# Routing weight rows by wide products, and FFN block 5's down side stacked in its idle rows

## The chip, the cores and the metric

The kernel runs on one core of a Trainium2 chip. The metric is the device time of one execution in microseconds. Engines: TensorE (PE), VectorE (DVE), ScalarE (ACT), GpSimd (POOL) and SyncE (SP, which only issues the loads and stores).

## What is computed

The reference is a four-stage transformer step on x of 1024 x 256 in fp32; every stage adds its output to x:

```python
x = x + attention(layernorm(x))
x = x + ffn(layernorm(x))
x = x + mixer(layernorm(x))      # state-space mixer
x = x + ffn(layernorm(x))        # the same weights as the first
```

The FFN is a mixture of 8 LoRA experts over one dense FFN with 704 hidden units. Each token picks the two experts with the highest router logits; the softmax that weighs them runs over all tokens of a choice (axis 1), so it needs a maximum and a sum over all 1024 tokens:

```python
topw, sel = top_k(x @ gate_w.T, 2)
topw = softmax(topw, axis=1)                     # over the tokens
for e in range(8):
    c = sum(where(sel == e, topw, 0.0))
    h_e = silu(base_up + lo_up[e]) * (base_gate + lo_gate[e])
    ch = c * h_e
    mixed_h += ch
    lora_down += 2 * (ch @ down_A[e].T @ down_B[e].T)
out = mixed_h @ w_down.T + lora_down
```

## The kernel before

All four stages are written out instruction by instruction for each engine, with semaphores between them; there is no planner. Engines run their own queues in the order in which the code issues to them. The FFN is built twice by `ffn(tag, first, before)`, for stage 2 and stage 4; only the first time are its weights split.

**Precision.** An fp32 product is made of three fp32r products: each operand is split into a high part (rounded to fp32r) and a low part (the remainder), and `three()` (L170 issues all its products) adds high x high, high x low and low x high. ACT writes high parts, DVE low ones.

**Tiling.** The 704 hidden units are cut into HB = 6 blocks of 128, the tokens into two halves of 512. A step i = 0..11 is one block in one half, i = HB * half + block. Block 5 has only 64 real units. Its up and gate results share one PSUM bank (`to_bank`): rows 0 to 63 up, rows 64 to 127 gate, so its base stage has 6 products in place of 12. ACT moves silu to rows 64 to 127, and the down weights of block 5 lie in rows 64 to 127 with zeros in rows 0 to 63. It is called packed.

**A step on PE.** `base_x(i)`: 12 products of 512 columns (up and gate, two halves of the model dimension, three terms). `base_lora(i)`: 6 products that add the first choice's LoRA; `second(i)`: 6 that add the difference between the second and the first choice's LoRA on top, once the first choice has been read. `down(i)`: for each of the two slots (choices) 3 products of 512 columns with down_A, and for each of 4 token tiles 3 products of 256 columns with w_down. Loop over i: base_x(i), base_lora(i), second(i-1), down(i-2). In step 8 lora_down(0) stands between second and down, and down(6) waits for the residual add of half 0.

**A step on ACT and DVE.** For each slot s: silu on ACT (L1140), `gated` on DVE (L1243, t = gate * silu, reads PSUM), `slot` (L1299, ch = t * weights wb), ACT's high part of ch (L1158), DVE's low part (L1310); then mix = ch of slot 0 + ch of slot 1 (L1306), its high part (L1169) and low part (L1318). base_x(i) waits for gated(i-2, 1). DVE also makes, in between, the masked LoRA inputs `masked` (L1255, 8 for each half, those of half 1 in steps 5 and 6), in the first FFN the low parts of the weights (`split`, L878), and in steps 8 to 12 work for the next stage (statistics and normalisation of half 0, low parts of the mixer's weights).

**Routing weights.** The chain is `top` on DVE, a transpose, a maximum, two small products on PE, exp on ACT, a sum on PE (L1037), reciprocal and product on DVE (L1283): WT, 128 x 16, one column for each slot and token tile. `weigh(h)` (L1018) spreads it over the partitions: one fp32 product of 128 columns for each slot and tile, with a column of WT as the stationary operand, broadcast to 128 columns, and the identity as the moving one; 8 a call, each two records in the trace. ACT copies the two banks to wb (`weights_out`, L1149). weigh(0) follows second(0), weigh(1) follows base_x(2).

**GpSimd** has in the FFN only the reciprocal square roots of the layer norms (L224).

Of the kernel before, what the change touches and what calls it, by code (L numbers as in the profile page):

```python
# [20 lines left out]
F32 = mybir.dt.float32  # L21
# [63 lines left out]
PR_END = PR_CS + 26  # L85
# [17 lines left out]
def build(nc, ins, out, phases=4):  # L103
    ctx = ExitStack()
    with ctx:
# [166 lines left out]
        def attention():  # L272
# [511 lines left out]
            def banks_free(e):  # L784
# [15 lines left out]
        s_fwh, s_fwl = sem("ffn_w_hi"), sem("ffn_w_lo")  # L800
# [6 lines left out]
        F_EVENTS = dict(lg=2, lgt=2, lgr=2, lgc=2, m8=NT, ix=NT, ixf=2, hot=4, top_dve=6, top_pe=3, ex=SLOTS,  # L807
                        wb=4, wbc=4, u=4, uhi=4, ulo=4, mk=4, mk0=2, mk1=2, mk2=2, um=16,
                        da=4, dd0=4, dd=4, dh=4, dl=4, y=4, add=4)
        F_EVENTS |= {n: 2 * HB for n in "a b d sil0 sil1 t0 t1 ch0 ch1 mix mxh mxl".split()} | dict(chh=4 * HB, chl=4 * HB)  # L810
        FS = {n: sem(f"ffn_{n}") for n in F_EVENTS}
        TOP_DVE = {n: i + 1 for i, n in enumerate(("mt", "gm", "dg", "nmc", "rs", "wt"))}
        TOP_PE = {n: i + 1 for i, n in enumerate(("mtT", "nm", "sum"))}

        def ffn(tag, first, before):
# [16 lines left out]
            d_hl = at(f"{tag}_d_hl", [P, 2, HALF], F32R, U_CH + 18432)  # L832
            lg = small[:, 0:64]
# [5 lines left out]
            WT = sm[:, 32:48].rearrange("p (k t) -> p k t", k=2)  # L839
# [116 lines left out]
            MASK_STEP = HB - 2  # L956

# [16 lines left out]
            def to_bank(i, which):  # L974
                return bank(i % 2 if i % HB == HB - 1 else 2 * which + i % 2)

            def base_x(e, i, parts=(0, 1)):
                h, b = divmod(i, HB)
# [21 lines left out]
            def pe(e):  # L1000
                def second(i):
                    h, b = divmod(i, HB)
                    if b == 0:
# [7 lines left out]
                def weigh(h):  # L1011
                    need(e, "top_dve", TOP_DVE["wt"])
# [25 lines left out]
                base_lora(e, 0)  # L1038
                base_lora(e, 1)
# [3 lines left out]
                def down(i):  # L1043
                    h, b = divmod(i, HB)
# [55 lines left out]
            def act(e):  # L1100
# [26 lines left out]
                split(3)  # L1127
                a_hi(1, (0,))
# [5 lines left out]
                def silu(i, s):  # L1134
# [3 lines left out]
                    packed = i % HB == HB - 1  # L1138
# [1076 lines left out]
```

## Time and profile before

| | us |
|---|---|
| Median of 3 runs (lowest to highest) | 546.32 (546.05 to 546.50) |
| The profiled execution, its own time | 543.31 |
| Its span in the trace | 541.50 |
| PE busy | 517.0 |
| DVE busy | 402.6 |
| ACT busy | 310.8 |
| POOL busy | 127.1 |

The stages by the timeline of PE, from the span's start: attention to about 207 us, the first FFN to 331, the mixer to 420, the second FFN to the end. In a row of a timeline the first number is the start, the second the length; a bracket gives the idle time of that engine before it and what ended it. Neighbouring instructions of a kind are merged (x12 is twelve of them). PE's ends are modelled and overlap what follows, so its pace is read from start to start.

### The profile page before, as it was taken

How to read it: one execution, taken by the hardware profiler on the slowest of the kernel's cores; microseconds unless marked ns; L12 is line 12 of the kernel's file. 1: busy time of each engine (PE TensorE's matmuls, PEld its weight loads, DVE VectorE, ACT ScalarE, POOL GpSimd, SP SyncE). 2: the span in 40 equal slices, each digit the busy share in tenths (PEclk: the TensorE clock that was granted, in tenths of full speed). 3: DMA queues.
4: the chain of work that ended last, by engine and by line, in shares of the span. 5: the costliest groups of instructions: out<-in, count | busy, mean ns of one | idle time of the engine just before them, and what ended most of it. 6: DMA issues, size and time to landing. Idle time of an engine off the chain costs nothing. (4 is left out here: it accounts for less than half of the span.)

```text
span 541.5 us, 9132 instructions
## 1 busy us (share of the span) xinstructions
PE 517.0 (95%) x3035; PEld 436.8 (81%) x3037; DVE 402.6 (74%) x899; ACT 310.8 (57%) x768; POOL 127.1 (23%) x272
## 2 busy tenths in 40 slices
PE   5999999999999989999999999999898999999996
PEld 4778899998998977788887888757777778888885
DVE  5625565566566898799987899966886877898767
ACT  3656878588687643573443455889662254443342
POOL 2232424244243310000000004569533100000000
PEclk9999999999999999999999999999999999999999
DMA  7320100000002204000040000000000000000101
GB/s 273 116 79 1 40 2 2 2 0 2 2 2 70 83 1 142 1 1 1 0 137 0 2 1 0 2 0 2 0 1 2 0 1 1 1 1 0 40 1 39
DMA packets 5790, 14.25 MB, mean 26 GB/s; under 512 B 624, under 2 KB 2928, under 8 KB 5744
## 3 DMA queue, kind: packets, MB, share of 16 engines
q1 hardware_dynamic: 5744, 13.66, 7.3%
q8 instruction: 25, 0.41, 0.3%
q14 instruction: 21, 0.17, 0.1%
HBM read 12.61 MB, written 1.05 MB: 25 GB/s over the span
## 5 line engine op out<-in xcount | busy, mean ns | idle before, releaser
L170 PE MATMUL psum<-xT_hl,ffn_w_hl 128*128 128x512 f32 x312 | 77.7, 395 | 0.6 <-DVE f_t L1243 0.4
L170 PE MATMUL psum<-f_um,ffn_w_hl 128*128 128x512 f32 x288 | 72.2, 398 | 1.3 <-DVE f_t L1243 1.3
L170 PEld LDWEIGHTS psum<-xT_hl,ffn_w_hl 128*128 128x128 f32 x312 | 56.2, 188 | 12.2 <-issue 0.9
L170 PEld LDWEIGHTS psum<-f_um,ffn_w_hl 128*128 128x128 f32 x288 | 53.3, 188 | 14.2 <-DVE f_um L1255 2.1
L1140 ACT ACTIVATE f_sil<-psum 128x512 f32<-128x512 f32 (+1 forms) x48 | 28.6, 596 | 60.3 <-PE psum L170 60.0
L170 PE MATMUL psum<-wo_hl,oT_hl 128*128 128x256 f32 x384 | 50.8, 281 | 4.2 <-DVE oT_hl L705 2.6
L699 DVE TENSOR_TENSOR pT_hl<-psum,pT_hl 126x360 fp32r<-126x360 f32 (+1 forms) x44 | 23.6, 537 | 41.4 <-ACT pT_hl L606 41.4
L170 PEld LDWEIGHTS psum<-wo_hl,oT_hl 128*128 128x128 f32 x384 | 47.9, 188 | 7.1 <-DVE oT_hl L705 5.1
L170 PE MATMUL psum<-xT_hl,wq_hl 128*128 128x512 f32 x192 | 52.1, 407 | 0.6 <-ACT qT L572 0.6
L1243 DVE TENSOR_TENSOR f_t<-psum,f_sil 128x512 f32<-128x512 f32 (+1 forms) x48 | 33.2, 691 | 26.2 <-ACT f_sil L1140 25.4
L572 ACT ACTIVATE qT<-psum 128x512 f32<-128x512 f32 x32 | 35.0, 1094 | 29.0 <-PE psum L170 29.0
L1158 ACT ACTIVATE f_ch_hl<-f_ch 128x512 fp32r<-128x512 f32 x48 | 30.2, 630 | 37.0 <-DVE f_ch L1299 36.9
L581 ACT ACTIVATE probs<-probs,small 120x66 f32<-120x66 f32 x120 | 40.7, 349 | 4.2 <-DVE small L682 3.4
L170 PEld LDWEIGHTS psum<-xT_hl,wq_hl 128*128 128x128 f32 x192 | 33.9, 189 | 7.7 <-issue 1.7
L170 PEld LDWEIGHTS psum<-ffn_w_hl,f_mix_hl 128*128 128x128 f32 x288 | 36.8, 188 | 3.3 <-DVE x_resid L1342 1.2
L170 PE MATMUL psum<-f_ch_hl,ffn_w_hl 128*128 128x512 f32 x144 | 37.9, 397 | 0.6 <-DVE f_ch_hl L1310 0.6
L170 PE MATMUL psum<-ffn_w_hl,f_mix_hl 128*128 128x256 f32 x288 | 37.7, 280 | 0.5 <-DVE x_resid L1342 0.5
L755 POOL TENSOR_TENSOR probs_wide<-probs,small 120x186 f32<-120x186 f32 x40 | 20.0, 499 | 65.8 <-DVE small L662 65.5
L224 POOL TENSOR_TENSOR ln_rstd<-ln_var_eps,minus_half 128x4 f32<-128x4 f32 x8 | 8.1, 1012 | 113.9 <-DVE ln_var_eps L217 113.9
L1299 DVE TENSOR_TENSOR f_ch<-f_t,f_wb 128x512 f32<-128x512 f32 x48 | 33.2, 691 | 1.4
L170 PEld LDWEIGHTS psum<-f_ch_hl,ffn_w_hl 128*128 128x128 f32 x144 | 26.6, 188 | 7.0 <-DVE f_ch_hl L1310 1.0
L1310 DVE TENSOR_TENSOR f_ch_hl<-f_ch,f_ch_hl 128x512 fp32r<-128x512 f32 x48 | 31.1, 686 | 0.0
(242 smaller groups left out, 1121.4 us busy)
## 6 DMA issues: line engine op xcount, KB each, us to landing
w_raw<-in_wq SPq DMA_DIRECT2D x4, 512.0 KB, 3.3
w_raw<-in_wo SPq DMA_DIRECT2D x4, 512.0 KB, 3.3
ffn_w_raw<-in_ffn SPq DMA_DIRECT2D x3, 576.0 KB, 5.6
ffn_w_raw_far<-in_ffn SPq DMA_DIRECT2D x3, 576.0 KB, 5.2
ssd_w_raw<-in_ssd SPq DMA_DIRECT2D x3, 512.0 KB, 5.7
x_resid<-in_x SPq DMA_DIRECT2D x2, 512.0 KB, 4.4
out_x<-x_resid SPq DMA_DIRECT2D x4, 256.0 KB, 2.2
w_raw<-in_wk SPq DMA_DIRECT2D x1, 512.0 KB, 6.3
```

What stands on the lines that cost most here:

```text
L170: i = e.matmul(dst, lhs(a), rhs(b), start=start and n == 0, stop=stop and n == len(TERMS) - 1, **kw)
L224: e.tensor_tensor(rstd[:, seg], veps[:, seg], minus_half[:, seg], ALU.pow).then_inc(LN["rstd"], 1)
L572: e.activation(qT[:, HALF * half:HALF * half + HALF, h], bank(7 if n == Q_PAIR else 6), ACT.Copy, scale=float(HD) ** -0.5).then_inc(s_qt, 1)
L581: m = e.activation(p[:, n, :], p[:, n, :], ACT.Exp, bias=NEGM[0:rows, u % 4, n:n + 1], accum_out=DEN[0:rows, u % 4, n:n + 1])
L699: e.tensor_tensor(pT_hl[0:nk, u % 2, LO, 0:n], bank(2 + u % 2)[0:nk, 0:n], f32(pT_hl[0:nk, u % 2, HI, 0:n]), ALU.subtract).then_inc(s_plo, 1)
L755: e.tensor_tensor(wide, p[:, :, SINK:KBLK], spread(r, KB_WIN), ALU.mult)
L1140: e.activation(sil[at_rows, s, :], bank(i % 2)[rows, :], ACT.Silu).then_inc(FS[f"sil{s}"], 1)
L1158: e.activation(ch_hl[:, i % 2, s, HI, :], ch[:, i % 2, s, :], ACT.Copy).then_inc(FS["chh"], 1)
L1243: e.tensor_tensor(tt[rows, s, :], to_bank(i, 1)[rows, :], sil[rows, s, :], ALU.mult).then_inc(FS[f"t{s}"], 1)
L1299: e.tensor_tensor(ch[:, i % 2, s, :], tt[:, s, :], wb[:, s, half(h)], ALU.mult).then_inc(FS[f"ch{s}"], 1)
L1310: e.tensor_tensor(ch_hl[:, i % 2, s, LO, :], ch[:, i % 2, s, :], f32(ch_hl[:, i % 2, s, HI, :]), ALU.subtract).then_inc(FS["chl"], 1)
```

## The change

**Weight rows.** DVE writes the weights repeated over 128 columns (w_rep); PE transposes them in one transpose, between base_lora(0) and base_lora(1); ACT copies the result (wr) and DVE subtracts it in the rows where the low part belongs (so wr holds high parts in some rows and low parts in others, by a column of parameters). For each half the rows are then spread into wr_rhs, four 128x128 products with a column of parameters, on ACT for half 0 and on POOL for half 1. slot_rows are two constant 128x128 tiles, made by ACT. weigh(h) becomes one product of 512 columns for each slot.

**Order of DVE around it.** masked(0, 4, 5), then the subtract, gated(0, 0), and only then masked(0, 6, 7); second(0) waits for the former before its first three products and for the latter before its other three.

**Block 5's down side.** Its down weights stand in both halves of the rows. Rows 0 to 63 of the high part are overwritten, once, with the low parts (ACT, at step 4 of the first FFN). POOL zeroes rows 0 to 63 of t before the step, and copies ch and mix from rows 64 to 127 into rows 0 to 63 of the low tiles. So two products in place of three give all three terms: the down products of block 5 are 2 x 2 and 4 x 2 in place of 2 x 3 and 4 x 3.

**Order of blocks.** In half 1: 0, 1, 2, 5, 3, 4; packed steps are 5 and 9 in place of 5 and 11.

**Waits.** base_x(i) waits, before its up products, only for silu(i-2, 1), unless step i-2 is packed, and for gated(i-2, 1) before its gate products. DVE's slot(i) waits in packed steps for the zeroing, and slot and mixed two steps later for POOL's copies; down in packed steps waits for them too. In the mixer two semaphores are merged into others, with the same waits.

The core of the diff:

```diff
+            ORDER = list(range(HB)) + [0, 1, 2, HB - 1] + list(range(3, HB - 1))
+            PACKED = [i for i in range(N) if ORDER[i] == HB - 1]
 def to_bank(i, which):
-    return bank(i % 2 if i % HB == HB - 1 else 2 * which + i % 2)
+    return bank(i % 2 if i in PACKED else 2 * which + i % 2)
 def base_x(e, i, parts=(0, 1)):
-                if i >= 2:
-                    need(e, "t1", i - 1)
                 for which in parts[:1] if b == HB - 1 else parts:
+                    if i >= 2:
+                        need(e, "t1" if which or i - 2 in PACKED else "sil1", i - 1)
 def second(i):
-                    if b == 0:
-                        need(e, "um", 8 * h + 8)
+                    if i % HB == 0:
+                        need(e, "um", 8 * h + 6)
                     need(e, "t0", i + 1)
                     for which in range(2):
+                        if i % HB == 0 and which:
+                            need(e, "um", 8 * h + 8)
 def weigh(h):
-                        for i in range(HT):
-                            t = HT * h + i
-                            m = e.matmul(bank(wb_bank(h, s))[:, i * P:(i + 1) * P],
-                                         WT[:, s, t:t + 1].broadcast_to([P, P]), ident, start=True, stop=True)
-                        m.then_inc(FS["wb"], 1)
+                        e.matmul(bank(wb_bank(h, s)), slot_rows[:, s, :], wr_rhs[:, h].rearrange("p t n -> p (t n)"),
+                                 start=True, stop=True).then_inc(FS["wb"], 1)
 # PE, start of the FFN
                 base_lora(e, 0)
+                need(e, "top_dve", TOP_DVE["wt"])
+                e.transpose(bank(7)[:, 2 * P:3 * P], w_rep, ident).then_inc(FS["top_pe"], 1)
                 base_lora(e, 1)
 def down(i):
+                        if i in PACKED:
+                            if s == 0:
+                                e.wait_ge(s_fwx, 1)
+                            need(e, "cx", 2 * h + s + 1)
+                            for w in (HI, LO):
+                                m = e.matmul(bank(6 + s), blk(HI, b, FB_DA, ER), ch_hl[:, i % 2, s, w, :],
+                                             start=False, stop=closes and w == LO)
...
+                        if i in PACKED:
+                            for w in (HI, LO):
+                                m = e.matmul(bank(4 + t // 2)[:, (t % 2) * D:(t % 2 + 1) * D],
+                                             mix_hl[:, i % 2, w, t * P:(t + 1) * P], blk(HI, b, FB_DN, D),
+                                             start=False, stop=False, skip_group_check=True)
+                            continue
 # ACT, start of the FFN
                 a_hi(1, (1,))
+                need(e, "top_pe", TOP_PE["wT"])
+                e.activation(wr, bank(7)[:, 2 * P:3 * P], ACT.Copy).then_inc(FS["wrh"], 1)
                 silu(0, 0)
+                need(e, "top_dve", TOP_DVE["wlo"])
+                for t in range(HT):
+                    m = e.activation(wr_rhs[:, 0, t, :], f32(wr), ACT.Copy, scale=par[:, WR_HALF + t:WR_HALF + t + 1])
+                m.then_inc(FS["wr0"], 1)
 # DVE, start of the FFN
-                masked(0, 4, 5, 6, 7)
+                masked(0, 4, 5)
+                need(e, "wrh", 1)
+                e.scalar_tensor_tensor(out=wr, in0=f32(wr), scalar=par[:, CS_LO:CS_LO + 1], in1=bank(7)[:, 2 * P:3 * P],
+                                       op0=ALU.mult, op1=ALU.add).then_inc(FS["top_dve"], 1)
                 gated(0, 0)
+                masked(0, 6, 7)
 def pool(e):
                 ln["rstd"](e, 1)
+                need(e, "top_dve", TOP_DVE["wlo"])
+                for t in range(HT):
+                    m = e.tensor_scalar(wr_rhs[:, 1, t, :], f32(wr), par[:, WR_HALF + HT + t:WR_HALF + HT + t + 1], None,
+                                        ALU.mult)
+                m.then_inc(FS["wr1"], 1)
+
+                def zeros(h, s):
+                    need(e, f"ch{s}", PACKED[h])
+                    e.memset(tt[0:REST, s, :], 0.0).then_inc(FS["z"], 1)
+
+                def stacked_rows(h):
+                    i = PACKED[h]
+                    need(e, "z", 2 * h + 2)
+                    need(e, "d", i - 1)
+                    for s in range(SLOTS):
+                        need(e, f"ch{s}", i + 1)
+                        e.tensor_copy(ch_hl[0:REST, i % 2, s, LO, :], ch[REST:P, i % 2, s, :]).then_inc(FS["cx"], 1)
+                        need(e, "cx", 2 * h + s + 1)
+                    need(e, "mix", i + 1)
+                    e.tensor_copy(mix_hl[0:REST, i % 2, LO, :], mix[REST:P, i % 2, :]).then_inc(FS["mx"], 1)
+                    need(e, "mx", h + 1)
+
+                zeros(0, 0)
+                zeros(0, 1)
+                stacked_rows(0)
+                zeros(1, 0)
                 early(phase, "rstd0", e)
+                zeros(1, 1)
+                stacked_rows(1)
```

## Rows read from the trace of the kernel before

**Rows 1.** Page: busy us, share of span, instructions of each engine

```profile
PE 517.0 (95%) x3035; PEld 436.8 (81%) x3037; DVE 402.6 (74%) x899; ACT 310.8 (57%) x768; POOL 127.1 (23%) x272
```

**Rows 2.** Windows, first FFN: length, busy PE, PEld, DVE, ACT, POOL; clock

```profile
236.00:330.00 94.00, 93.09 (x489) 78.15 (x488) 83.23 (x148) 43.06 (x76) 1.01 (x1) 1.00 0.06 20
```

**Rows 3.** Timeline of PE, an ordinary block: start us, length us

```profile
240.29 2.93 PE L170 MATMUL psum<-xT_hl,ffn_w_hl 128*128 128x512 f32 x12
243.06 2.96 PE L170 MATMUL psum<-f_um,ffn_w_hl 128*128 128x512 f32 x12
245.86 1.56 PE L170 MATMUL psum<-f_ch_hl,ffn_w_hl 128*128 128x512 f32 x6
247.26 1.56 PE L170 MATMUL psum<-ffn_w_hl,f_mix_hl 128*128 128x256 f32 x12
248.66 2.89 PE L170 MATMUL psum<-xT_hl,ffn_w_hl 128*128 128x512 f32 x12
```

**Rows 4.** Timeline of PE, second FFN: weigh(0) and what comes after it

```profile
441.01 1.95 PE L1018 MATMUL psum<-const_f,softmax_small 128*128 128x128 f32 x16
442.71 3.01 PE L170 MATMUL psum<-xT_hl,ffn_w_hl 128*128 128x512 f32 x12
```

**Rows 5.** Groups by line, transposes: busy us, mean ns, idle before

```profile
L238 PE MATMUL psum<-const_f,xn 128*128 128x128 f32 x24 | 3.7, 287 | 0.1
```

**Rows 6.** Page, costliest groups: DVE's low parts of ch

```profile
L1310 DVE TENSOR_TENSOR f_ch_hl<-f_ch,f_ch_hl 128x512 fp32r<-128x512 f32 x48 | 31.1, 686 | 0.0
```

**Rows 7.** Timeline, second FFN's start: gated(0,0) on DVE, second(0) on PE

```profile
438.71 0.69 DVE L1243 TENSOR_TENSOR f_t<-psum,f_sil 128x512 f32<-128x512 f32 x1
439.54 1.63 PE L170 MATMUL psum<-f_um,ffn_w_hl 128*128 128x512 f32 x6 [0.66 <-DVE f_t L1243]
```

**Rows 8.** Timelines of DVE and PE, first FFN

```profile
229.19 0.69 DVE L1243 TENSOR_TENSOR f_t<-psum,f_sil 128x512 f32<-128x512 f32 x1 [1.19 <-ACT f_sil L1140]
...
236.04 0.69 DVE L1318 TENSOR_TENSOR f_mix_hl<-f_mix,f_mix_hl 128x512 fp32r<-128x512 f32 x1 [0.31 <-ACT f_mix_hl L1169]
...
253.62 0.69 DVE L1243 TENSOR_TENSOR f_t<-psum,f_sil 128x512 f32<-128x512 f32 x1 [0.45 <-ACT f_sil L1140]
...
271.77 0.69 DVE L1243 TENSOR_TENSOR f_t<-psum,f_sil 64x512 f32<-64x512 f32 x1
...
272.91 2.89 PE L170 MATMUL psum<-xT_hl,ffn_w_hl 128*128 128x512 f32 x12
...
277.87 0.69 DVE L1243 TENSOR_TENSOR f_t<-psum,f_sil 128x512 f32<-128x512 f32 x1 [2.08 <-ACT f_sil L1140]
...
290.31 1.68 PE L170 MATMUL psum<-ffn_w_hl,f_mix_hl 128*128 128x256 f32 x12 [0.48 <-DVE x_resid L1342]
...
300.75 3.00 PE L170 MATMUL psum<-xT_hl,ffn_w_hl 128*128 128x512 f32 x12 [0.43 <-DVE f_t L1243]
```

**Rows 9.** Timelines of DVE and PE, second FFN

```profile
457.94 0.69 DVE L1243 TENSOR_TENSOR f_t<-psum,f_sil 128x512 f32<-128x512 f32 x1 [2.18 <-ACT f_sil L1140]
...
484.42 0.70 DVE L1243 TENSOR_TENSOR f_t<-psum,f_sil 64x512 f32<-64x512 f32 x1
...
485.56 2.89 PE L170 MATMUL psum<-xT_hl,ffn_w_hl 128*128 128x512 f32 x12
...
533.00 0.96 PE L170 MATMUL psum<-f_ch_hl,ffn_w_hl 128*128 128x512 f32 x3 [0.59 <-DVE f_ch_hl L1310]
```

**Rows 10.** Groups by line and shape on POOL, the mixer

```profile
L2010 POOL TENSOR_SCALAR mask_f32r<-const_f 128x512 fp32r<-128x512 f32 x1 | 0.6, 617 | 0.1
...
L1971 POOL TENSOR_SCALAR xs_D<-xs,params 128x512 f32<-128x512 f32 x6 | 9.9, 1642 | 0.0
...
L2022 POOL TENSOR_SCALAR cumsum_sel<-cumsum_hl,params 128x128 fp32r<-128x128 f32 x8 | 3.6, 447 | 0.0
```

**Rows 11.** Timeline, mixer: a GpSimd product and DVE's g_lo

```profile
378.32 1.05 POOL L2046 TENSOR_TENSOR x_dt_decay<-x_dt,decay 128x512 f32<-128x512 f32 x1
378.61 1.30 DVE L1908 TENSOR_TENSOR g_lo<-gated,g_hi 128x512 fp32r<-128x512 f32 x1 [0.87 <-ACT g_hi L1838]
```

More of the change, by code:

```diff
@@ L832, in ffn @@
             d_hl = at(f"{tag}_d_hl", [P, 2, HALF], F32R, U_CH + 18432)
+            wr = at(f"{tag}_weight_rows", [P, P], F32R, A_W + 16384)[:, :]
+            w_rep = at(f"{tag}_weights_repeated", [P, P], F32, A_W + 16896)[:, :]
+            slot_rows = at(f"{tag}_slot_rows", [P, SLOTS, P], F32R, A_W + 17408)
+            wr_rhs = at(f"{tag}_weight_rows_rhs", [P, 2, HT, P], F32R, A_W + 20480)
             lg = small[:, 0:64]
@@ L1047, in down @@
                         need(e, "ulo", 4)
-                    if h == 1 and b == 0:
+                    if h == 1 and opens:
                         need(e, "dd0", 2)
@@ L1127, in act @@
                 split(3)
+                for n in range(SLOTS):
+                    e.activation(slot_rows[:, n, :], ones, ACT.Copy, scale=par[:, WR_SLOT + n:WR_SLOT + n + 1])
                 a_hi(1, (0,))
@@ L1198, in act @@
                         split(6, 7)
+                    if i == MASK_STEP and first:
+                        e.wait_ge(s_fwl, HB + 1)
+                        stacked = slice(F_BLK + (HB - 1) * FB + FB_DN, F_BLK + HB * FB)
+                        e.activation(w_hl[0:REST, HI, stacked], f32(w_hl[0:REST, LO, stacked]),
+                                     ACT.Copy).then_inc(s_fwx, 1)
                     if i == N - 5:
@@ L1240, in gated @@
                         need(e, f"ch{s}", i)
-                    packed = i % HB == HB - 1
+                    packed = i in PACKED
                     rows = slice(REST, P) if packed else slice(0, P)
@@ L1309, in lo_slot @@
                     need(e, "chh", 2 * i + s + 1)
-                    e.tensor_tensor(ch_hl[:, i % 2, s, LO, :], ch[:, i % 2, s, :], f32(ch_hl[:, i % 2, s, HI, :]),
-                                    ALU.subtract).then_inc(FS["chl"], 1)
+                    rows = slice(REST, P) if i in PACKED else slice(0, P)
+                    e.tensor_tensor(ch_hl[rows, i % 2, s, LO, :], ch[rows, i % 2, s, :],
+                                    f32(ch_hl[rows, i % 2, s, HI, :]), ALU.subtract).then_inc(FS["chl"], 1)
                 def lo_parts(i):
@@ L1317, in lo_parts @@
                     need(e, "mxh", i + 1)
-                    e.tensor_tensor(mix_hl[:, i % 2, LO, :], mix[:, i % 2, :], f32(mix_hl[:, i % 2, HI, :]),
-                                    ALU.subtract).then_inc(FS["mxl"], 1)
+                    rows = slice(REST, P) if i in PACKED else slice(0, P)
+                    e.tensor_tensor(mix_hl[rows, i % 2, LO, :], mix[rows, i % 2, :],
+                                    f32(mix_hl[rows, i % 2, HI, :]), ALU.subtract).then_inc(FS["mxl"], 1)
                 def lora_mask(h):
@@ L2177, in pack @@
                     blocks(padh(eb(a["ffn_up_B"]), 1), P), blocks(behind(eb(a["ffn_gate_B"]), 1), P),
[L2178 to L2179 removed]
+                    kmaj(twice(a["ffn_w_down"])).transpose(1, 0, 2),
+                    kmaj(twice(er(a["ffn_down_A"]))).transpose(1, 0, 2))
     ffn = [kmaj(er(a["ffn_up_A"])), kmaj(er(a["ffn_gate_A"]))] + [w for b in per_block for w in b] + [eb(a["ffn_down_B"])]
```

94 lines of the change are left out of this document (58 added, 36 removed).

## The prediction, made before the changed kernel was run

> **What bounds the kernel now.** I read the page's engine table first: TensorE (PE) is busy 95% of the span, VectorE (DVE) 74% [rows 1]. A share says nothing of single stages, so I took the table by windows: from 236 to 330 us, nearly all of the first FFN, PE is busy 93.09 of 94.00 us and DVE 83.23 [rows 2]. PE bounds it, but DVE is close behind. The timeline of PE then shows how work is paced. One ordinary block is 12 base products, 12 LoRA products, 6 down-A products and 12 down products, back to back with no idle note: 2.77, 2.80, 1.40 and 1.40 us from start to start [rows 3]. So a product with 512 columns costs 0.233 us and one with 256 columns 0.117. The clock is 1.00 in the window [rows 2], the 2.4 GHz level, and the change makes no pause in PE long enough that I expect that to differ.
>
> **What leaves PE.** (a) Weight rows: weigh() is 8 fp32 products of 128 columns, 16 in the records, and takes 442.71 - 441.01 = 1.70 us [rows 4]; there are four such calls, two in each FFN. After, each is two 512-column products: 2 x 0.233 = 0.47. Saved 4 x 1.23 = 4.9 us. (b) New are two transposes of 128x128; 24 such take 3.7 us [rows 5], so 0.15 each, 0.3 together. (c) Block 5's down side: per half two products of 512 columns and four of 256 fall away, 0.47 + 0.47 = 0.93; four halves make 3.7 us. (d) Order 0,1,2,5,3,4 in half 1: block 5's short base stage (6 products, 1.4 us less) comes two iterations earlier; the sum is unchanged. PE would save 4.9 - 0.3 + 3.7 = 8.3 us. My forecast is far less, because much of this lands where DVE or a chain through it sets the time.
>
> **FFN start.** The transpose goes in after base_lora(0); behind it on ACT come the copy into wr, silu(0,0) and four copies that make wr_rhs for half 0; on DVE the subtract for the low rows (an op of DVE with two SBUF inputs and 512 columns occupies 31.1/48 = 0.65 us [rows 6], so 128 columns at most that) waits for that copy. Queued behind the subtract is gated(0,0), which PE's second(0) waits for. Today gated(0,0) starts at 438.71 right behind four masked products and second(0) at 439.54 after 0.66 idle [rows 7]. Tomorrow only two masked products precede it (1.3 less), the subtract and the ACT detour are added (up to 1.3 more): I leave it at its time, with bounds -1.3 and +0.7. The other two masked products come behind it: ready at 438.71 + 0.69 + 1.3 = 440.7, whereas PE has done three of six products at 439.54 + 0.70 = 440.24. PE waits 0.4, so second(0) and gated(0,1), which follows it through ACT's silu, come 0.4 later. base_x(2) came 1.70 after second(0), with weigh(0) between; now it waits, in its first half, for silu(0,1) alone, some 0.8 after second(0) (0.65 as for such an op, and the hand-over), so it starts 0.9 - 0.4 = 0.5 earlier. Two constant copies on ACT (slot_rows), the one copy that stacks block 5's low weights and the four for half 0's rows find room: ACT is busy 43.06 of 94.00 us [rows 2]; without that room they cost up to 0.65 each. The parameter load grows by ten columns, at a point where nothing waits for it; no load is added.
>
> **First FFN.** DVE runs without idle from gated(0,1) at 229.19 to gated(4,0), but for 0.31 at 236.04 (waiting for ACT) and 0.45 at 253.62 (waiting for silu) [rows 8]. PE's 2 x 1.23 arrive early at a DVE that can't start earlier: DVE is 0.4 late, wins 0.31 (weights_out(1) leaves ACT earlier) and 0.45, net 0.35, and then runs full until gated(5,1) at 271.77, for which base_x(7) waits; that today starts 0.45 after it ends (272.91 - 272.46) [rows 8]. So at base_x(7) PE gains 0.8, not 2.4. Here silu's earlier release doesn't help, because block 5 holds both its results in one bank. Next, down(5) is 0.93 shorter, but the down stage of iteration 8 already waits 0.48 for the residual add of DVE (290.31) [rows 8]; it will wait 1.4. Still 0.8. The 0.43 stall before base_x(10) (gated(8,1), 300.75) goes, as the first half needs only silu: 1.2. The early base stage lends 1.4 and takes it back at base_x(11). down(9)'s 0.93 does count, for DVE started that stretch 1.4 earlier: 2.2 us at the end of this FFN. It is then carried through the mixer unchanged: only semaphore names differ there.
>
> **Second FFN.** No weight splits here, so DVE idles 2.18 before gated(3,0) [rows 9]. PE keeps 1.23 (weigh(1)) + 0.5 (base_x(2)) = 1.75. base_x(7) starts at 485.56, 0.44 after gated(5,1) ends (485.12) [rows 9], and both shift alike. down(5)'s 0.93 goes into the wait for add(0), as in the first. down(9)'s goes too: the tail is a DVE chain from gated(11,0) on, and PE already waits 0.59 for its last ch_hl at 533.00 [rows 9]. So 1.75. Together 3.95 us if GpSimd's new work is free.
>
> **What GpSimd's work costs.** Each packed half adds two memsets (64x512) and three copies (64x512, crossing partitions); each FFN start adds four products of 128x128. No row has a copy across partitions. The nearest one-input op with 512 columns took 0.617 us, the same with a scalar per partition 1.64 [rows 10]; I take 0.62 and keep 1.64 as the bound (below, 0.3: half of it, as half the partitions). A 128x128 product takes 0.447 [rows 10]. Waits of DVE for them (ch(7), mixed(7), ch(11)) and of PE's down(5), down(9) come an iteration later and are covered by over 2 us, but engines also collide: DVE's g_lo, two SBUF inputs, started at 378.61 while GpSimd's product from 378.32 to 379.37 ran, and took 1.30 against 0.69 for such an op; it ended 0.54 after GpSimd did [rows 6, 11]. So DVE stands still until GpSimd has finished. The Trainium skill ("SBUF — State Buffer", Who interferes with whom) has it as an exclusive lock: a DVE op with two SBUF inputs and a GpSimd op that reads SBUF block each other fully, whichever started second; that row agrees. The new memsets only write and by the same section don't collide; no row here shows it.
>
> Nearly all DVE ops around the new copies have two SBUF inputs. Where DVE is a full chain, a block costs the whole op: in each FFN start two masked products may be held by 0.45 each; in the first FFN the first copy of half 0 (0.62) is in the chain, and of half 1 two copies (1.24), of which 0.6 is covered (DVE's lead of 1.4 less down(9)'s 0.93, and some hand-over); those after step 5 meet the 2.08 before 277.87 [rows 8]; in the second FFN the first copy meets 0.44 of slack (0.18), and the others meet idle time. Fully blocked: 0.9 + 0.9 + 0.62 + 0.64 + 0.18 = 3.2. Never blocked: 0. No row says who wins when DVE has the next op waiting, so I take one hit of two: 0.45 + 0.45 + 0.3 + 0.1 + 0 = 1.3. Forecast: 3.95 - 1.3 = 2.65 us. The profiled run took 543.31 (span 541.5), 3.0 below the median of 546.32; subtracted from the median this gives 543.7.
>
> **Rivals.**
> *PE keeps its saving* (0.12): the DVE waits dissolve because ops shift by fractions. For it: PE is 99% busy in [rows 2]. Against: DVE's chain in [rows 8] is unbroken. 5 to 8.3 us: 538.0 to 541.3, middle 539.7.
> *Every copy blocks* (0.14): 3.95 - 3.2 = 0.75, 545.6. The rule of the page above, a lock for the whole op, would give this if GpSimd always comes in between two DVE ops.
> *The copy across partitions is dear* (0.07), slower: with c per copy and full blocking, 3.95 - 1.8 leaves 2.15; the chain copies cost 3c - 0.6 in the first FFN and c - 0.44 in the second, so the gain is 3.2 - 4c. It turns at c = 0.8, and at 1.64 [rows 10] is -3.4: 549.7.
> *It doesn't do what it says* (0.05): second(0) waits for masked products and ACT for as long as weigh saves: 546.3.
> The forecast has 0.62.
>
> **Numbers.** Measurement can tell about 0.2%, 1.1 us. Faster: 0.62 + 0.12 + 0.03 of the full-block case (parts of it under 545.2) = 0.77; same: 0.11 + 0.05 = 0.16; slower 0.07. The range runs from 541.0 (forecast without any collision, 542.4, and a little of the first rival) to 546.3 (takes in full blocking and the last rival).
>
> **What would show it.** L1018's 64 records gone, four pairs of 512-column products at about 0.47 a call; 3.7 us less of down products. PE's idle grows at second(0) (0.4 for f_um), base_x(7) and the adds (about 1.4), and at 533 (1.5); DVE's ch, mixed and lo ops, always 0.69 today, show some of 1.0 to 1.3 beside GpSimd's copies. If PE has no such new idle, the DVE part of my reading is wrong; if copies last over 1 us, their price is.

## The result, and the profile of the changed kernel

Six runs of each kernel: before 545.10 us (median; three of the six are those that the forecast started from), after 539.02 us, ratio 0.9897 (95%: 0.9874 to 0.9921). The forecast was 543.7, range 541.0 to 546.3. The direction was right; the gain was larger than forecast, and the time lies below the range. Runs of either kernel come at two levels, 1.4 to 2.5 us apart (the last section shows where part of that arises), and those three runs all lay on the upper one; so I compare traces first. The profiled run took 538.82 us against 543.31 with full clock in both, and the spans differ by 541.5 - 537.0 = 4.5 us. Forecast: 2.65.

The page's engine line and two groups of after, to hold against [rows 1] and [rows 6]; the third is the new zeroing on POOL:

```profile
PE 510.3 (95%) x2957; PEld 427.7 (80%) x2959; DVE 407.6 (76%) x901; ACT 313.3 (58%) x783; POOL 149.5 (28%) x300
...
L1367 DVE TENSOR_TENSOR f_ch_hl<-f_ch,f_ch_hl 128x512 fp32r<-128x512 f32 (+1 forms) x48 | 35.6, 779 | 0.1
...
L1463 POOL MEMSET f_t<- 64x512 f32 x8 | 4.2, 520 | 101.6 <-DVE f_ch L1353 101.6
```

PE is busy for 6.7 us less, DVE for 5.0 more. 4.5 of that is one group: the low parts of ch, 31.1 us in [rows 6], now 35.6, though not one was added and some cover half the partitions. That is the collision with GpSimd, sized below.

The timeline of PE at the first FFN's start (start us, length us, engine, line, operation, count, and in brackets the idle time before it and what ended it):

```profile
226.58 0.94 PE L172 MATMUL psum<-f_um,ffn_w_hl 128*128 128x512 f32 x3 [0.27 <-DVE f_t L1284]
227.78 0.96 PE L172 MATMUL psum<-f_um,ffn_w_hl 128*128 128x512 f32 x3 [0.27 <-DVE f_um L1296]
228.58 0.61 PE L1028 MATMUL psum<-f_weight_rows_rhs,f_slot_rows 128*128 128x512 f32 x2
229.52 3.01 PE L172 MATMUL psum<-xT_hl,ffn_w_hl 128*128 128x512 f32 x12 [0.33 <-ACT f_sil L1170]
232.37 0.62 PE L1028 MATMUL psum<-f_weight_rows_rhs,f_slot_rows 128*128 128x512 f32 x2
232.83 1.56 PE L172 MATMUL psum<-f_um,ffn_w_hl 128*128 128x512 f32 x6
```

Weigh costs 232.83 - 232.37 = 0.46 us (forecast 0.47; 1.70 in [rows 4]). second(0) waits once for gated(0,0) and once for the masked inputs, and base_x(2), which is now held by silu alone, waits 0.33. Around block 5 and the two steps that follow it:

```profile
271.72 3.00 PE L172 MATMUL psum<-xT_hl,ffn_w_hl 128*128 128x512 f32 x12 [0.53 <-DVE f_t L1284]
274.56 2.96 PE L172 MATMUL psum<-f_um,ffn_w_hl 128*128 128x512 f32 x12
277.36 1.10 PE L1069 MATMUL psum<-f_ch_hl,ffn_w_hl 128*128 128x512 f32 x4
278.30 1.09 PE L1084 MATMUL psum<-ffn_w_hl,f_mix_hl 128*128 128x256 f32 x8
279.23 2.89 PE L172 MATMUL psum<-xT_hl,ffn_w_hl 128*128 128x512 f32 x12
...
285.71 1.65 PE L172 MATMUL psum<-ffn_w_hl,f_d_hl 128*128 128x256 f32 x12 [0.79 <-DVE f_d_hl L1393]
...
289.23 1.67 PE L172 MATMUL psum<-ffn_w_hl,f_mix_hl 128*128 128x256 f32 x12 [0.47 <-DVE x_resid L1400]
```

down(5) takes 279.23 - 277.36 = 1.87 instead of 2.80, as forecast. Its 0.93 turns into idle time at once: 0.79 + 0.47 = 1.26 before the two products that wait for DVE in step 8, where [rows 8] has 0.48 (I forecast 1.4).

DVE and POOL in the same stretch:

```profile
264.35 1.70 DVE L1367 TENSOR_TENSOR f_ch_hl<-f_ch,f_ch_hl 128x512 fp32r<-128x512 f32 x2
...
270.88 0.69 DVE L1284 TENSOR_TENSOR f_t<-psum,f_sil 64x512 f32<-64x512 f32 x1
271.61 0.69 DVE L1353 TENSOR_TENSOR f_ch<-f_t,f_wb 128x512 f32<-128x512 f32 x1
272.39 0.69 DVE L1362 TENSOR_TENSOR f_mix<-f_ch 128x512 f32<-128x512 f32 x1
273.11 2.01 DVE L1367 TENSOR_TENSOR f_ch_hl<-f_ch,f_ch_hl 64x512 fp32r<-64x512 f32 x2
```

```profile
225.70 4.26 POOL L1457 TENSOR_SCALAR f_weight_rows_rhs<-f_weight_rows,params 128x128 fp32r<-128x128 f32 x4 [15.47 <-DVE f_weight_rows L1332]
...
264.29 0.61 POOL L1471 CAST f_ch_hl<-f_ch 64x512 fp32r<-64x512 f32 x1
272.43 1.12 POOL L1471 CAST f_ch_hl<-f_ch 64x512 fp32r<-64x512 f32 x1 [7.53 <-DVE f_ch L1353]
273.62 0.96 POOL L1474 CAST f_mix_hl<-f_mix 64x512 fp32r<-64x512 f32 x1
```

For the whole study I cut the span into three stages by PE's timeline: the first FFN from its first base product to the first z product of the mixer, the mixer to the first LoRA product of the second FFN, and that to the last group of LoRA down products. Before: 119.72, 109.25, 100.67. After: 117.47, 109.09, 98.68. So the gain is 2.25 + 0.16 + 1.99.

### The profile page after: what moved, and what is told of

It reads as the page before. It is cut to its first block and busy times, and to the rows that moved or that the text cites. A ratio compares the mean times of both kernels' runs of the same rounds, so it can differ in the third digit from the quotient of the medians.

```text
span 537.0 us, 9053 instructions
## 1 busy us (share of the span) xinstructions
PE 510.3 (95%) x2957; PEld 427.7 (80%) x2959; DVE 407.6 (76%) x901; ACT 313.3 (58%) x783; POOL 149.5 (28%) x300
## 3 DMA queue, kind: packets, MB, share of 16 engines
HBM read 12.62 MB, written 1.05 MB: 25 GB/s over the span
## 5 line engine op out<-in xcount | busy, mean ns | idle before, releaser
L1367 DVE TENSOR_TENSOR f_ch_hl<-f_ch,f_ch_hl 128x512 fp32r<-128x512 f32 (+1 forms) x48 | 35.6, 779 | 0.1
L172 PEld LDWEIGHTS psum<-ffn_w_hl,f_mix_hl 128*128 128x128 f32 x240 | 30.7, 188 | 3.6 <-DVE x_resid L1400 1.8
L172 PE MATMUL psum<-f_ch_hl,ffn_w_hl 128*128 128x512 f32 x120 | 31.7, 398 | 1.1 <-DVE f_ch_hl L1367 1.1
L1463 POOL MEMSET f_t<- 64x512 f32 x8 | 4.2, 520 | 101.6 <-DVE f_ch L1353 101.6
L172 PE MATMUL psum<-ffn_w_hl,f_mix_hl 128*128 128x256 f32 x240 | 31.5, 280 | 0.9 <-DVE x_resid L1400 0.9
L172 PE MATMUL psum<-pT_hl,v_hl 126*128 126x360 f32 (+1 forms) x132 | 30.4, 339 | 0.0
```

Of the source, the lines that this page charges most:

```text
L172: i = e.matmul(dst, lhs(a), rhs(b), start=start and n == 0, stop=stop and n == len(TERMS) - 1, **kw)
L1367: e.tensor_tensor(ch_hl[rows, i % 2, s, LO, :], ch[rows, i % 2, s, :], f32(ch_hl[rows, i % 2, s, HI, :]), ALU.subtract).then_inc(FS["chl"], 1)
L1463: e.memset(tt[0:REST, s, :], 0.0).then_inc(FS["z"], 1)
```

## The experiments

Each was timed beside the kernel before. The table has the ratio to it with its interval, and the stages in us from one profile each. A star marks a profile in which the clock was low at the end of the mixer; the FFN stages aren't touched by that and are what I compare.

| run | ratio (95%) | first FFN | mixer | second FFN |
|---|---|---|---|---|
| c_after | 0.9912 (0.9895-0.9930) | 117.49 | 109.20 | 98.71 |
| x_no_pool_reads | 0.9902 (0.9880-0.9924) | 116.61 | 110.62* | 98.33 |
| x_copies_doubled | 0.9958 (0.9944-0.9973) | 118.57 | 110.82* | 99.07 |
| w_weigh_only | 0.9920 (0.9902-0.9938) | 117.48 | 109.33 | 98.75 |
| s_stack_only | 0.9973 (0.9956-0.9990) | 118.66 | 110.71* | 100.52 |
| r_no_early_release | 0.9970 (0.9951-0.9988) | 119.14 | 110.69* | 99.42 |
| e_release_only | 1.0006 (0.9988-1.0023) | 119.04 | 110.88* | 100.68 |
| w_no_release | 0.9961 (0.9941-0.9982) | 119.19 | 110.84* | 99.49 |
| o_natural_order | 1.0000 (0.9979-1.0021) | 119.31 | 110.84* | 100.52 |
| m_masked_first | 0.9932 (0.9908-0.9957) | 117.96 | 109.14 | 99.07 |
| v_act_copies | 0.9898 (0.9881-0.9915) | 116.69 | 109.08 | 98.46 |
| v_defer | 0.9895 (0.9872-0.9917) | 116.12 | 109.15 | 97.68 |
| v_act_defer | 0.9868 (0.9849-0.9888) | 115.27 | 109.17 | 97.44 |
| v_act_defer_mask | 0.9854 (0.9830-0.9877) | 115.06 | 110.61* | 97.54 |

c_after is the changed kernel again: its FFN stages come out within 0.03 us of the first profile's, the only measure here of how far two profiles of one kernel differ.

> The changed kernel itself once more, beside the kernel before on one chip, as the base of the comparisons. The two traces differ by 4.5 us in their spans, the first ratio says 5.6 with an interval from 4.3 to 6.9. If the spans tell the truth, the ratio comes out near 0.9917 (4.5 us less); if there is a gain that the traces don't show, near 0.990.

The ratio, 0.9912, is 4.8 us less than before. That is near the 4.5 of the traces (0.9917); its interval just takes in 0.990 too. The 0.9897 above leans on the three high runs of before.

**GpSimd without reads.** The copies and the four products become memsets of the same size, so POOL still works but reads nothing. Left out by that: block 5's low terms on the down side and half 1's routing weights.

```diff
-e.tensor_copy(ch_hl[0:REST, i % 2, s, LO, :], ch[REST:P, i % 2, s, :])
+e.memset(f32(ch_hl[0:REST, i % 2, s, LO, :]), 0.0)
...
-m = e.tensor_scalar(wr_rhs[:, 1, t, :], f32(wr), par[...], None, ALU.mult)
+m = e.memset(f32(wr_rhs[:, 1, t, :]), 1.0)
```

> GpSimd's three copies of each packed block and its four products of each FFN start are replaced by memsets of the same tiles with the same waits, so it reads nothing there; the low terms of block 5 and half 1's routing weights are left out. By the collisions as the prediction charged them (1.3 us in all, up to 3.2) this is at least 1.3 us faster than the changed kernel. By the trace of the changed kernel, where DVE lost 0.1 at each FFN start and 0.41 + 0.72 at each packed block, most of it ahead of an idle stretch of DVE, it is 0.3 to 0.8 faster.

DVE and POOL of this run, in the stretch shown above:

```profile
265.15 1.29 DVE L1367 TENSOR_TENSOR f_ch_hl<-f_ch,f_ch_hl 128x512 fp32r<-128x512 f32 x2
...
273.51 1.29 DVE L1367 TENSOR_TENSOR f_ch_hl<-f_ch,f_ch_hl 64x512 fp32r<-64x512 f32 x2
```

```profile
272.81 0.52 POOL L1470 MEMSET f_ch_hl<- 64x512 f32 x1 [7.21 <-DVE f_ch L1353]
273.60 0.52 POOL L1473 MEMSET f_mix_hl<- 64x512 f32 x1 [0.27 <-DVE f_mix L1362]
```

The second pair of low parts starts 0.09 before a memset and takes 1.29, where it took 2.01 beside a copy; the first takes 1.29 instead of 1.70. So a write alone doesn't hold DVE, and a copy, which also reads, does: 0.41 + 0.72 for each packed block. Over the four packed blocks that is 4.5 us of DVE's time, all that the group of low parts grew by. Little of it reaches the end: the first FFN gets 117.47 - 116.61 = 0.86 shorter, the second 98.68 - 98.33 = 0.35. The collisions cost 1.2 us, against 1.3 charged, and more than the 0.3 to 0.8 that I expected of this run. And the gain without them is 3.11 + 2.34 = 5.45 (from 119.72 and 100.67), not 3.95. So a term failed in the part that I took for certain.

**Copies twice.** Each copy is issued twice, each with its own count.

```diff
 e.tensor_copy(ch_hl[0:REST, i % 2, s, LO, :], ch[REST:P, i % 2, s, :])
+need(e, "cx", 2 * (2 * h + s) + 1)
+e.tensor_copy(ch_hl[0:REST, i % 2, s, LO, :], ch[REST:P, i % 2, s, :])
```

> Each of GpSimd's copies in a packed block is done twice. If the copies cost the time that the prediction charged for full blocking (0.62 each where DVE is a full chain), this is 1.4 us or more slower than the changed kernel, for four chain copies are added. If DVE loses only parts that idle stretches take up again, 0.2 to 0.8 slower.

1.10 us longer in the first FFN and 0.39 in the second, 1.5 together: what full blocking asks for (1.4 or more), and not the 0.2 to 0.8 of a DVE that makes up for it. PE shows it where base_x(7) waits for gated of block 5, 0.53 in the changed kernel:

```profile
272.38 1.85 PE L172 MATMUL psum<-xT_hl,ffn_w_hl 128*128 128x512 f32 x7 [0.95 <-DVE f_t L1284]
```

The two runs agree: a copy costs time mainly in the first FFN, where DVE is nearly full, some 0.9 to 1.1 for six of them, and 0.4 in the second.

**One part of the change alone.** w_weigh_only keeps the wide weight rows and silu's early release, but block 5 stays last with three-term products, and POOL zeroes and copies nothing. s_stack_only has weigh, WT and the masked order of before; it stacks block 5 and keeps the new block order and the early release.

```diff
# w_weigh_only
-ORDER = list(range(HB)) + [0, 1, 2, HB - 1] + list(range(3, HB - 1))
+ORDER = 2 * list(range(HB))
...
-if i in PACKED:
+if False:
...
# s_stack_only
-e.matmul(bank(wb_bank(h, s)), slot_rows[:, s, :], wr_rhs[:, h]...)
+m = e.matmul(bank(wb_bank(h, s))[:, i * P:(i + 1) * P], WT[:, s, t:t + 1].broadcast_to([P, P]), ident, ...)
...
-masked(0, 4, 5) ... gated(0, 0); masked(0, 6, 7)
+masked(0, 4, 5, 6, 7); gated(0, 0)
```

> Only the wide weight rows, with the order of work around them and the earlier bank release; block 5's down side and the block order are as before. If PE bounds everywhere, 4.6 us less than before (4 x 1.23 less two transposes). By the DVE chain: 0.8 to 1.2 at base_x(7) of the first FFN, 0.4 at base_x(10), 1.8 in the second FFN, so 3.0 to 3.5 us less than before.

> Only block 5's stacked down side, the order 0,1,2,5,3,4 in half 1 and the earlier bank release; the weight rows by narrow products as before. If PE bounds everywhere: 4 x 0.93 = 3.7 us less than before. By the DVE chains: the 0.93 of down(5) goes into the wait for the residual add in both FFNs, that of down(9) counts in the first FFN alone, and the stall at base_x(10) goes (0.4), less what the first copy costs: 0.8 to 1.4 us less than before.

Weigh with the release gives 2.24 + 1.92, nearly all that the whole change gives (2.25 + 1.99) and above the 3.0 to 3.5 expected by the DVE chain. Stacking with the release gives 1.06 + 0.15; the release alone gives 0.68 and -0.01 (e_release_only, below), so stacking and its order have 0.38 + 0.16 of that. On top of weigh, stacking adds 0.01 + 0.07: its own saving (without POOL's reads 117.48 - 116.61 = 0.87 and 98.75 - 98.33 = 0.42) is about what the collisions, 0.86 + 0.35, take back.

**Silu's early release.** The up products of base_x wait for gated again.

```diff
-need(e, "t1" if which or i - 2 in PACKED else "sil1", i - 1)
+need(e, "t1", i - 1)
```

> The changed kernel with base_x waiting for gated(i-2, 1) before its first product, as before. My working gives the earlier release 0.5 us at base_x(2) and 0.4 at base_x(10) of the first FFN, and 0.5 at base_x(2) of the second, of which the first is lost to the DVE chain: 0.8 to 1.0 us slower than the changed kernel. If the release is worth nothing, as the 1.3 us of idle before these products in the trace of before suggests for single waits, under 0.3.

```profile
231.24 2.97 PE L172 MATMUL psum<-xT_hl,ffn_w_hl 128*128 128x512 f32 x12 [1.05 <-DVE f_t L1284]
...
240.83 2.52 PE L172 MATMUL psum<-xT_hl,ffn_w_hl 128*128 128x512 f32 x10 [0.55 <-DVE f_t L1284]
```

base_x(2) waits 1.05 instead of 0.33, base_x(3) 0.55 where it waited for nothing, and base_x(10) has its wait back (0.54; 0.43 in [rows 8]). The stages lose 1.67 + 0.74 = 2.4 us. That is more than I gave it (0.9 at base_x(2), less 0.4, and 0.43 at base_x(10)). Two more runs settled how they combine: the release added to the kernel before, and taken from w_weigh_only.

```diff
# e_release_only, on before
-if i >= 2:
-    need(e, "t1", i - 1)
 for which in parts[:1] if b == HB - 1 else parts:
+    if i >= 2:
+        need(e, "t1" if which or (i - 2) % HB == HB - 1 else "sil1", i - 1)
# w_no_release, on w_weigh_only: the edit of r_no_early_release
```

> The kernel before with the earlier bank release alone. The trace of before has 0.43 of idle ahead of base_x(10) in the first FFN and none of over 0.1 ahead of the other base products. If the release is worth what those idle notes say, 0.4 us in the first FFN and nothing in the second. If it starts PE's products of a whole chain earlier by itself, over 1 us.

> Only the wide weight rows, without the earlier release (block 5 and the order as before). If the two parts are worth what they are worth alone, the FFNs are 0.4 us longer together than with the release (4.2 us less than before), so 3.8 less. If the release is what lets PE use the time that the weight rows save, because base_x(2) and base_x(3) otherwise wait for gated(0, 1) and gated(1, 1), about 2.4 us longer than with it: 1.8 us less than before, which is what the changed kernel without it showed.

By stages: the release alone gives 0.68 and nothing (0.01 longer), wide rows alone 0.53 + 1.18, the two together 2.24 + 1.92. So 1.03 and 0.75 us exist only with both. Weigh stood between second(0) and base_x(2) and covered the wait for gated(0,1); shorter, it lays the wait bare, as w_no_release shows, and only the release then turns the saving into time:

```profile
230.83 2.99 PE L172 MATMUL psum<-xT_hl,ffn_w_hl 128*128 128x512 f32 x12 [1.04 <-DVE f_t L1282]
```

This base_x(2) stands 23.37 us behind the FFN's start, 0.17 later than in the kernel before, in spite of the 1.23 saved; base_x(3) is 0.47 earlier, and 1.88 earlier in the changed kernel.

**Order.** Block 5 stays last in half 1.

```diff
-ORDER = list(range(HB)) + [0, 1, 2, HB - 1] + list(range(3, HB - 1))
+ORDER = 2 * list(range(HB))
# POOL: the zeroing for half 1 moves behind the layer norm's root
+early(phase, "rstd0", e)
 zeros(1, 0)
-early(phase, "rstd0", e)
```

> The changed kernel with block 5 last in half 1 (packed steps 5 and 11). If the order matters: in the tails down(11) then waits for copies behind the last mix, and its shorter products stand in a stretch that DVE bounds, so 0.9 us of the first FFN's gain goes and up to 1 us is added in the second, 0.9 to 2 us slower than the changed kernel. If the order is free, within 0.3.

The tail of this run, and below it that of after:

```profile
534.37 0.73 PE L1069 MATMUL psum<-f_ch_hl,ffn_w_hl 128*128 128x512 f32 x2 [1.65 <-DVE f_ch_hl L1367]
535.39 1.21 PE L1084 MATMUL psum<-ffn_w_hl,f_mix_hl 128*128 128x256 f32 x8 [0.29 <-DVE f_mix_hl L1376]
538.17 1.64 PE L172 MATMUL psum<-ffn_w_hl,f_d_hl 128*128 128x256 f32 x12 [1.57 <-DVE f_d_hl L1393]
```

```profile
528.74 0.96 PE L172 MATMUL psum<-f_ch_hl,ffn_w_hl 128*128 128x512 f32 x3 [0.82 <-DVE f_ch_hl L1367]
...
532.12 1.64 PE L172 MATMUL psum<-ffn_w_hl,f_d_hl 128*128 128x256 f32 x12 [0.99 <-DVE f_d_hl L1393]
```

The stages are 1.84 us longer in each FFN (119.31 - 117.47, 100.52 - 98.68), 3.7 together, where I expected 0.9 to 2. w_weigh_only has block 5 last too, without stacking, and is as short as the changed kernel; so it is not the short block in the last place that costs, but the stacked one (119.31 - 117.48 and 100.52 - 98.75). DVE's last two low parts of this run show why:

```profile
533.33 0.99 DVE L1367 TENSOR_TENSOR f_ch_hl<-f_ch,f_ch_hl 64x512 fp32r<-64x512 f32 x1
534.24 1.10 DVE L1376 TENSOR_TENSOR f_mix_hl<-f_mix,f_mix_hl 64x512 fp32r<-64x512 f32 x1
```

In the last block everything hangs on DVE's chain. POOL's copies run beside these two (such operations take 0.69 elsewhere), and PE, with 0.93 less to do in the packed down stage, only waits longer. Behind them DVE reaches the last step before the final products here, and in w_weigh_only, at:

```profile
535.37 1.29 DVE L1384 SCALAR_TENSOR_TENSOR f_dd<-psum,f_mT 128x512 f32<-128x512 f32 x2
```

```profile
529.95 1.29 DVE L1376 SCALAR_TENSOR_TENSOR f_dd<-psum,f_mT 128x512 f32<-128x512 f32 x2
```

Counted from the start of this stage (437.65 and 434.00) that is 97.72 against 95.95, 1.77 later and all of the stage's loss. Of it 0.30 + 0.41 are the two rows above, 0.41 the copy before them (the pair of low parts takes 1.70), 0.2 was there at base_x(11), and about 0.35 is an idle stretch ahead of a mix that I haven't taken apart. My sum gave the order down(9)'s 0.93 in the first FFN and some cover for the copies, and nothing in the second; otherwise it "lends 1.4 and takes it back".

**Masked products first.** masked(0, 6, 7) in front of gated(0, 0), as in the kernel before.

```diff
-gated(0, 0)
 masked(0, 6, 7)
+gated(0, 0)
```

> The changed kernel with masked(0, 6, 7) ahead of gated(0, 0) again. Then second(0) starts 1.3 - 0.1 later but runs through: PE's two waits of 0.27 become one. By the chain through silu(0,1) the start of DVE's full stretch moves by the difference, 0.0 to 0.3 us later in each FFN: 0.1 to 0.6 slower. If the order of these is what gave the second FFN its gain, over 1 us slower.

```profile
228.46 1.63 PE L172 MATMUL psum<-f_um,ffn_w_hl 128*128 128x512 f32 x6 [1.25 <-DVE f_t L1284]
```

One wait of 1.25 instead of two of 0.27; the stages lose 0.49 and 0.39, more together than the 0.1 to 0.6 expected. So splitting the waits pays.

**Could it be better?** Three edits follow from the readings: the copies on ACT, behind mix's high part, instead of POOL; down(6) in two stages, its down_A part ahead of lora_down(0) and its w_down part behind base_x(9), so that the wait for the residual add is covered; and the masked inputs of half 1 made behind that step's low parts.

```diff
# v_act_copies, in ACT's step; stacked_rows taken from POOL
+if i in PACKED:
+    for s in range(SLOTS):
+        e.activation(ch_hl[0:REST, i % 2, s, LO, :], ch[REST:P, i % 2, s, :], ACT.Copy)
+    e.activation(mix_hl[0:REST, i % 2, LO, :], mix[REST:P, i % 2, :], ACT.Copy)
# v_defer, in PE's loop
 base_x(e, i)
+if i == HB + 3: down(HB, (1,))
...
 if i == HB + 2:
+    down(HB, (0,))
     lora_down(0)
...
-if i >= 2:
+if i >= 2 and i != HB + 2:
     down(i - 2)
# v_act_defer: both. v_act_defer_mask: both, and in DVE's loop
-if i == MASK_STEP + 2: masked(1, 4, 5, 6, 7)
 ... lo_parts(i - 1)
+if i == MASK_STEP + 2: masked(1, 4, 5, 6, 7)
```

> The changed kernel with the three copies of each packed block on ACT in place of GpSimd; the memsets and the four products of each FFN start stay on GpSimd. With the copies replaced by memsets the first FFN was 0.9 us and the second 0.4 us shorter than in the changed kernel, of which 0.1 each came from the four products. If it is the collision of GpSimd's reads with DVE that costs, this regains 0.8 to 1.1 us. If it is DVE waiting for the copied rows, or if ACT's extra 2 us per packed block come in the way of silu, it regains nothing or loses up to 1 us.

> The changed kernel with PE's order around the residual add changed: down(6)'s first part ahead of lora_down(0), its second part after base_x(9). The trace of the changed kernel has PE idle 0.79 + 0.47 there in the first FFN and about 0.1 + 0.48 in the second. If the add is what holds PE, and the 0.93 saved by down(5) is lost in it, this is 1.2 to 1.8 us faster, as base_x(9) fills the wait. If DVE's chain behind it sets the time anyway, under 0.3.

> Both of these together. If they are separate losses they add up: 2.0 to 2.9 us faster than the changed kernel. If both lie on one DVE chain, only the larger of the two.

> And, beyond both, DVE's masked(1, 4, 5, 6, 7) moved from ahead of gated(6, 0) to behind the low parts of step 5. base_x(7) then no longer waits 0.5 in the first FFN; second(6) needs the masked products about 4 us later. If that chain is what took the early gain of the weight rows (1.9 us at base_x(6), 1.2 at base_x(7)), another 0.2 to 0.6 us. If the products now come too late for second(6), it is slower by up to 1 us.

Against c_after the stages gain 0.80 + 0.25 by the copies on ACT, nearly what taking all reads away gave (0.88 + 0.38); DVE's low parts of ch are back at 31.1 us in all (35.6 in after), so ACT's copies cost DVE nothing. They gain 1.37 + 1.03 by the deferred down and 2.22 + 1.27 by both, more than the 1.8 and 2.9 that I expected at most. PE's timeline of v_act_defer has no idle note where after waited 0.79 and 0.47 (nor the 0.53 before base_x(7)):

```profile
282.73 2.96 PE L172 MATMUL psum<-f_um,ffn_w_hl 128*128 128x512 f32 x12
285.53 1.56 PE L172 MATMUL psum<-f_ch_hl,ffn_w_hl 128*128 128x512 f32 x6
286.93 1.56 PE L172 MATMUL psum<-ffn_w_hl,f_d_hl 128*128 128x256 f32 x12
288.33 1.53 PE L172 MATMUL psum<-xT_hl,ffn_w_hl 128*128 128x512 f32 x6
290.00 1.67 PE L172 MATMUL psum<-ffn_w_hl,f_mix_hl 128*128 128x256 f32 x12
```

The masked order adds 0.21 in the first FFN and costs 0.10 in the second: no difference can be claimed. v_act_defer (0.9868) and v_act_defer_mask (0.9854) have the lowest ratios of the study; v_act_defer's interval lies below c_after's 0.9895 to 0.9930.

## Why the prediction missed, step by step

**What held.** PE's prices (0.46 for weigh, 1.87 for the packed down stage). base_x(2) comes 0.56 and 0.52 us earlier than before, counted from the FFN's start; forecast 0.5. down(5)'s saving goes into the add wait in both FFNs: in the first, base_x(8) is 2.03 earlier and the down stage behind the add 1.10; in the second base_x(8) 2.64 and base_x(9) 1.75. The 0.43 before base_x(10) is gone. By the Trainium skill ("SBUF — State Buffer", Who interferes with whom) DVE operations with two SBUF inputs and GpSimd's reads exclude each other, and a memset, which only writes, doesn't. The runs agree: the pairs took 1.70 and 2.01 beside copies and 1.29 beside memsets. The copy across partitions took 0.61, as taken; the rival of a dear copy (turning at 0.8) is out: the 1.12 and 0.96 stand beside DVE's operations with two SBUF inputs.

**What came out right by luck.** The collisions cost 1.2 us, and I had charged 1.3, but for other things. I had 0.45 in each FFN for the products of 128x128 and 0.3 + 0.1 for all copies. v_act_copies takes the copies alone off GpSimd, and they cost 0.80 + 0.25 = 1.05; what is left to x_no_pool_reads, 0.08 + 0.13, is all that the products can have cost. One hit of two was too high for the products and too low for the copies.

**What failed first: "DVE runs without idle".** At base_x(7) I had -0.4 for DVE's late start, 0.31 + 0.45 for its two noted waits and 0.45 for the time that PE took behind gated(5,1): 0.8. Without POOL's reads base_x(7) came 1.70 earlier, and with them 1.21. The windows of the chain from gated(0,1) to gated(5,1), of before, of x_no_pool_reads and of after (length, then busy PE, PEld, DVE, ACT, POOL):

```profile
229.19:271.77 42.58, 42.58 (x229) 35.86 (x229) 40.58 (x69) 22.75 (x37) 0.00 (x0) 1.00 0.01 2
```

```profile
230.19:271.27 41.08, 40.96 (x210) 34.13 (x211) 40.02 (x69) 22.46 (x38) 1.56 (x3) 1.00 0.03 7
```

```profile
229.41:270.88 41.47, 41.36 (x213) 34.52 (x214) 40.41 (x70) 22.45 (x38) 2.20 (x4) 1.00 0.04 10
```

The term that was too small is this stretch. I gave it 0.76, and without collisions it is 42.58 - 41.08 = 1.50 shorter, with the same 69 operations. DVE's gaps shrink from 42.58 - 40.58 = 2.00 to 1.06, by 0.94: the noted 0.31 + 0.45, as forecast, and 0.18 of waits too short for a note. Its busy time shrinks by 40.58 - 40.02 = 0.56. Two low parts in a row take 1.29 and not 2 x 0.69: the record of one operation overlaps the next by some 0.08, and an operation that comes late loses this overlap, which no idle note shows. The 1.06 of gaps that stay are alike in all three runs, 0.03 before many operations and 0.09 to 0.10 before a mix, between operations of DVE itself; they were no slack. The rest of the step: gated(0,1) came 0.1 late and not 0.4 (22.43 behind the FFN's start, before 22.33), and PE's 0.45 behind gated(5,1) became 0.15. So -0.10 + 1.50 + 0.30 = 1.70. With the copies the stretch takes 0.39 more. This is the first rival's mechanism ("DVE waits dissolve because ops shift by fractions"), in part: the 5.45 us without collisions lies in its 5 to 8.3; with them the gain is below it.

**Second, the end of the first FFN.** From 0.8 at base_x(7) I came to 2.2 at the end; from 1.70 the run without reads came to 3.11. The 1.4 in between (0.43 at base_x(10), 0.93 of down(9)) is what I had.

**Third, the second FFN** was 1.75 without collisions; measured 2.34, and 1.99 with them. With them base_x(2) and base_x(3) have 0.52 and 1.85; without, the gain is 1.95 at base_x(3), 2.06 at base_x(9) and 2.34 at the end. So 0.2 to 0.3 more than my 1.75 is there ahead of the tail, and 0.3 comes in it. The sum counted nothing at the tail, taking the DVE chain there to swallow down(9)'s whole saving; it expected PE to wait 1.5 for the last low part, and the wait is 0.82. Which wait lets the 0.3 through I haven't taken apart.

**Fourth, the baseline.** 2.65 was worked out on a trace of 543.31 and subtracted from a median of 546.32. Taken from the trace's own time it would have been 540.7 against 538.82 measured, and the range 538.0 to 543.3. The text said how far the two are apart and then used the farther one. So of the 4.7 us between 543.7 and 539.02, 3.0 are the baseline, and it alone puts the time outside the range; the other part is the gain, 4.5 in place of 2.65. The median lies in the first rival's 538.0 to 541.3 through the same baseline.

**Not seen at all:** that wide rows and release are worth more together (about 1.8 us of 4.2), which is why one can't price them one by one; and that the order carries 3.7 us once block 5 is stacked.

## What to carry over

Where an engine's chain is read as full, the idle notes are not all its slack: hold the stretch against one in which the engine is fed in time. Here the same 69 operations took 42.58 us and then 41.08, and half of that showed in no note. Nor is every gap slack: 1.06 us of them stayed. A shortened stage pays only if the wait that it had covered is loosened as well, so price the edits in pairs and look at what each lays bare. Work given to GpSimd beside a busy VectorE costs what it reads there; where ScalarE has room, it is the better place. Here stacking brings 0.01 + 0.07 us with the copies on GpSimd and 0.79 + 0.29 with them on ScalarE (117.48 - 116.69, 98.75 - 98.46).

## What the runs showed of the hardware

**Both engines lose in a collision, in turns.** At 264.29 GpSimd's copy starts 0.06 before DVE's low part and takes its 0.61; DVE's pair takes 0.41 more. At 272.43 the copy starts 0.04 after a DVE operation has begun and takes 1.12; the next, at 273.62, 0.96; and DVE's pair loses 0.72. GpSimd's four products of 128x128 took 4.26 in the first FFN and 3.07 in the second, where four times 0.447 [rows 10] is 1.8, while DVE lost about 0.1 on its two masked products (1.38, and 1.28 in the kernel before). I had charged DVE for these; GpSimd paid, and no idle note of PE stands before the weigh that needs its rows.

**The clock at the end of the mixer.** In some runs TensorE's granted clock falls there, from 1.00 (2.4 GHz) towards the 1.2 GHz level, for a few us. x_no_pool_reads against after, windows (the 1.00 or 0.61 behind POOL's busy time is the granted clock):

```profile
412.00:416.00 4.00, 2.97 (x25) 2.73 (x24) 2.67 (x8) 2.12 (x4) 0.55 (x1) 0.96 0.02 4
416.00:420.00 4.00, 4.00 (x18) 3.64 (x17) 2.02 (x7) 0.00 (x0) 1.10 (x2) 0.61 0.00 0
```

```profile
416.00:420.00 4.00, 4.00 (x24) 3.45 (x23) 3.12 (x10) 0.50 (x1) 1.10 (x2) 1.00 0.00 0
```

Ahead of it PE did eight transposes, stood idle for 1.03 and did eight one-column products, in both runs alike:

```profile
414.55 1.05 PE L1791 MATMUL psum<-const_f,gated_sq 128*128 128x1 f32 x8 [1.03 <-DVE x_resid L2026]
...
416.06 0.41 PE L172 MATMUL psum<-ssd_w_out_hi,g_hi 128*128 128x256 f32 x1
```

A 256-column product takes 0.41 there instead of 0.28, and the mixer 110.6 to 110.9 instead of 109.1 to 109.3: 1.5 us. The starred runs of the table all have it. It is one reason why ratios of whole runs don't follow the stages: v_defer's stages are 2.4 us shorter than c_after's, its ratio only 0.0017 lower, and four of its six runs have a mean clock of 0.997 while its profile has 1.00. Another lies ahead of the first FFN, which begins at 206.86 to 208.18 us in these sixteen profiles, starred or not; why is open. What tips a run to one side or the other stays open; the work ahead of it is the same.
